# A two-layer attention, state-space and mixture kernel: the run-time loop over its batches written out

## The reference

```
x = x + attention(layernorm(x))      # A: linear attention, 16 heads of 8, a state that decays per token
x = x + mixture0(layernorm(x))       # B: top 2 of 8 experts, 352 hidden rows each, SiLU gated
x = x + state_space(layernorm(x))    # C: conv of width 3, selective scan with 16 states per feature, SiLU gate
x = x + mixture1(layernorm(x))       # D: top 2 of 8 experts, 128 hidden rows each, and 2 shared experts
```

## Time and profile before

| what | value |
|---|---|
| median of 3 runs | 2598.52 us (2598.12 to 2598.66) |
| span of the profiled execution, first to last instruction | 2595.4 us |
| PE busy | 2081.9 us, 80% |
| DVE busy | 1865.9 us, 72% |
| POOL busy | 1347.7 us, 52% |
| ACT busy | 1134.1 us, 44% |
| a turn of the loop, 922.34 to 1229.58 us | 307.24 us |

### The profile page before, as it was taken

The page is one execution under the profiler, slowest core; times in us unless marked ns, Lnnn a source line. Parts: engine busy times, 40 slices in busy tenths (PEclk is TensorE's granted clock), DMA queues, the critical chain, the costliest instruction groups (busy, mean ns, idle before and its releaser), DMA issues.

```text
span 2595.4 us, 26854 instructions
## 1 busy us (share of the span) xinstructions
PE 2081.9 (80%) x6944; PEld 866.6 (33%) x6944; DVE 1865.9 (72%) x3076; ACT 1134.1 (44%) x1491; POOL 1347.7 (52%) x848
## 2 busy tenths in 40 slices
PE   3589787789779987798877897878877998787468
PEld 1234332334323333233333343333332333332023
DVE  5655569775895859866697757967589676974972
ACT  1133374325644265243652347432663427535324
POOL 4346358453583537644485444745368353862343
PEclk8789899899898998899998999889988999988579
DMA  4000000000000000000000000000000000000000
GB/s 129 0 9 1 9 1 1 1 1 17 1 1 1 1 18 1 1 1 2 17 1 1 1 2 17 1 1 1 18 1 1 1 1 9 0 1 0 0 0 17
DMA packets 24911, 18.10 MB, mean 7 GB/s; under 512 B 2704, under 2 KB 23984, under 8 KB 24496
## 3 DMA queue, kind: packets, MB, share of 16 engines
q1 hardware_dynamic: 24752, 16.23, 2.0%
HBM read 12.04 MB, written 4.19 MB: 6 GB/s over the span
## 4 chain that ended last, share of the span: by engine, by line
PE 45%; issue 20%; DVE 17%; POOL 9%; ACT 7%; DVEq 1%; POOLq 0%; DMA 0%; ACTq 0%; SPq 0%
PE bank L920 10%; PE bank L780 7%; PE bank L782 7%; PE bank L781 6%; POOL mix_arena L746 4%; DVE arena L1303 4%; DVE arena L1314 3%; POOL arena L717 3%; PE bank L908 2%; PE bank L843 2%; DVE arena L1247 2%; PE bank L824 2%; DVE arena L1294 2%; POOL y L727 2%; PE bank L791 2%
## 5 line engine op out<-in xcount | busy, mean ns | idle before, releaser
L746 POOL TENSOR_TENSOR mix_arena<-mix_arena 128x512 f32<-128x512 f32 (+1 forms) x512 | 816.3, 1610 | 691.9 <-ACT mix_arena L1100 690.9
L1388 DVE SCALAR_TENSOR_TENSOR mix_arena<-bank,winv,mix_arena 128x512 f32<-128x512 f32 (+1 forms) x544 | 403.6, 744 | 436.0 <-PE bank L782 353.1
L1113 ACT ACTIVATE mix_arena<-bank,winv 128x512 f32<-128x512 f32 (+1 forms) x544 | 372.6, 687 | 575.3 <-PE bank L782 565.0
L920 PE MATMUL bank<-mix_arena,W_Bw 128*128 128x512 f32 (+1 forms) x768 | 432.9, 649 | 0.0
L727 POOL TENSOR_TENSOR y<-y,arena 128x1024 f32<-128x1024 f32 x120 | 284.1, 2367 | 199.2 <-DVE arena L1314 199.1
L1303 DVE TENSOR_TENSOR_SCAN arena<-arena 128x1024 f32<-128x1024 f32 x128 | 383.6, 2996 | 0.1
L780 PE MATMUL bank<-x_partsB,W_hi 128*128 128x512 f16 x712 | 298.7, 420 | 99.1 <-DVE mix_arena L1388 40.5
L876 PE MATMUL bank<-bc_parts,sel_bc 96*128 96x512 bf16 x512 | 198.4, 429 | 204.3 <-DVE arena L1314 162.4
L1100 ACT COPY mix_arena<-bank 128x512 f32<-128x512 f32 x256 | 149.6, 584 | 447.9 <-PE bank L908 447.7
L782 PE MATMUL bank<-x_partsB,W_lo 128*128 128x512 f16 x712 | 296.1, 416 | 0.0
L781 PE MATMUL bank<-x_partsB,W_hi 128*128 128x512 f16 x712 | 294.0, 413 | 0.0
(11 more groups left out here) (168 smaller groups left out, 2649.0 us busy)
## 6 DMA issues: line engine op xcount, KB each, us to landing
x<-in_x SPq DMA_DIRECT2D x8, 512.0 KB, 4.1
out<-x SPq DMA_DIRECT2D x8, 512.0 KB, 3.2
mix_arena<-in_W SPq DMA_DIRECT2D x2, 1408.0 KB, 8.4
W_Bw<-in_W SPq DMA_DIRECT2D x2, 512.0 KB, 14.2
mix_arena<-in_W SPq DMA_DIRECT2D x1, 640.0 KB, 11.3
x<-in_W SPq DMA_DIRECT2D x1, 640.0 KB, 12.4
W_Dw<-in_W SPq DMA_DIRECT2D x1, 640.0 KB, 4.9
x<-in_Wv SPq DMA_DIRECT2D x1, 512.0 KB, 4.4
```

The lines of the kernel that those rows point to most:

```text
L746: pool.tensor_tensor(slot, slot, g_ring[0:rows, q % RG, :], ALU.mult).then_inc(m_sg[s].sem, 1)
L920: last = pe.matmul(banks[4][:], W2[s][0:rows, i, :], h_ring[0:rows, k % RH, :], start=(i == 0), stop=(i == NT[s] - 1))
L1113: read(s, act.activation(s_ring[0:rows, k % RS[s], :], bank(s, f"a{k}", rows), ACT.Silu, scale=down[W1[s]][0:rows]))
L1388: read(s, dve.scalar_tensor_tensor(out=h_ring[0:rows, k % RH, :], in0=bank(s, f"b{k}", rows), scalar=down[W3[s]][0:rows], in1=s_ring[0:row ...
```

## The change

Both loops become Python loops, so that the body stands five times in each stream and every count is a constant:

```diff
-            with eng.Fori(1, B - 2) as i:
+            for i in range(1, B - 2):
                 ssm_beside(e, i, "B", i + 1, counts(A=i + 2, B=i + 1, C=i, D=i, PB=i + 2, PD=i), ("D", i),
                            ("D", i - 1), ("A", i + 2))
                 attention_beside(e, i + 2, "D", i, counts(A=i + 2, B=i + 2, C=i + 1, D=i, PB=i + 2, PD=i + 1),
...
             next_x(0)
             next_x(1)
-            with sp.Fori(0, B - 3) as b:
+            for b in range(0, B - 3):
                 store_x(b)
                 next_x(b + 2)
             for b in range(B - 3, B):
```

## The result

The kernel after takes 2571.71 us, median of four runs (2568.12 to 2572.78), against 2598.59 before (2598.12 to 2601.89): a ratio of 0.9893, 95% interval 0.9879 to 0.9907. The profiled execution (2568.12, span 2566.3) is the fastest of the four, 29.1 us off the profiled span of before.

What follows compares the result with a forecast made beforehand. No engine was full; PE and DVE waited for each other at every tile. Returns 10.3 plus registers 8.2, fetch and SP 0, gave 18.5 us off: 2598.5 - 18.5 = 2580.0 us, own range 2576 to 2583.5, with rivals 2575 to 2589.

Steps and rivals of the forecast that it cites:

- Part 1: Return to the loop's head, taken four times: 2.57 us each at the next mark, 10.3 us saved.
- J to N: From end of previous turn's gates (L1373) to the convolution's SiLU (L1042): 17.87 us with return, forecast 15.05 in turns 1 to 5.
- whole-turn figure: Turns 2 to 5 against turn 1, 307.18 against 303.98 us: 3.2 per return, upper bound 12.8.
- only the branch counts: Rival at the loop's head: a return costs only its branch, 0.3 us for four; 2590 us, chance 0.05.
- Part 2: Register instructions computing the waits' counts in the loop: 1.64 us a turn, 8.2 us over five.
- N to G: From the convolution's SiLU (L1042) to the product y times z (L1320): registers cost 0.90 us a turn.
- G to J: From the product y times z (L1320) to the gates' end (L1373): 139.69 to 139.20 us, 0.49 a turn.
- Part 3: Fetching the longer straight code instead of the loop: cost 0; a late fetch would cost 2.9 us.
- Part 4: SP's loop of one store and one load a turn: worth 0, upper bound under 0.2 us.
- Only the returns: Rival for the loop: register instructions are hidden, 10.3 to 12.8 us off, say 2587 us, chance 0.18.
- The clock: Something between, anywhere in the turns: a saving given back through a lower granted clock or different phase, chance 0.05.
- No DVE gap: Sign at the turns' borders: no DVE gap put down to issue at L1388, previously 2.92 us.

Runs made afterwards that it cites:

- m_pe: Kernel before with PE's stream written out, constants and no return; DVE, ACT and POOL keep loop and registers: 2597.87 us, ratio 0.9991.
- m_dve: Kernel before with DVE's stream written out, constants and no return; PE, ACT and POOL keep loop and registers: 2580.09 us, ratio 0.9926.
- e2_hint: Kernel before, loop and registers kept, with a hint to fetch the loop's head ahead: 2583.63 us, ratio 0.9938 to the kernel before.
- r_pe: Kernel after with counts computed in registers on PE alone, in once-run loops, no returns: 2586.43 us, ratio 0.9944 to the kernel before.
- e1_reg: Kernel after with counts computed in registers on all engines, each turn a once-run loop, no returns: 2585.84 us, ratio 0.995 to the kernel before.
- p10: Kernel after with DVE clearing 960 scratch columns at the end of turns 1 to 4: 2569.15 us, ratio 0.9878 to the kernel before.
- pb07: Kernel after with 0.75 us of DVE scratch clearing behind L1282 in turns 1 to 5: 2565.57 us, ratio 0.9877 to the kernel before.
- fill_b: Kernel before with 14 zero-weight products on PE where it idles for POOL in the attention scan: 2591.85 us, ratio 0.9972.
- r_ap: Kernel after with counts computed in registers on ACT and POOL alone, no returns: 2563.73 us, ratio 0.9885 to the kernel before.
- p28: Kernel after with DVE clearing 2700 scratch columns at the end of turns 1 to 4: 2607.77 us, ratio 1.0037 to the kernel before.

## Why the prediction was wrong

The direction, the order of the parts and the mechanism at the border were right; the size was not, and it fell outside the range.

**Part 1, returns.** The mechanism holds: fetch of the target, DVE's gap above PE's (m_pe has 17.7 to 18.0 us from J to N, m_dve 16.5 to 16.6), 2.57 us at mark N. J to N saved 11.2 us over the five turns where 10.3 + 1.25 were forecast. What was mis-sized is the step from a mark to a turn: the term 4 x 2.57 = 10.3 measured 13 to 16 by the ratios. The whole-turn figure, 3.2 and at most 12.8 in all, was there and I kept it as a bound; e2_hint's turn is 3.4 us shorter than that of before, and its time 16 us. The rival that only the branch counts, with 0.3 us for four returns, falls by the same 16 us.

**Part 2, registers.** Forecast 8.2, measured 12 to 15. The failed step is that turn 0 was the reference for code without registers. N to G was to fall by 0.90 and fell by 2.0 a turn, G to J by 0.49 and fell by 1.1. Turn 0 was one draw: W to S15 there took 111.4 us before and 113.9 after, A0 to A15 45.0 and 42.7, with instructions that are the same. A reference that itself moves by over 2 us in a stretch can't price 0.9. What stands without doubt is the 0.5 a turn in N to W and S15 to G for all engines together, 2.5 us; the rest appears in the two scans, where the clock's drops stand. Of these the attention scan is shown to follow the clock, 1.3 a turn; for the state-space scan, 1.5 a turn, that is not shown. The bounds were taken from DVE's ALU_OPs of two lines alone, 205 a turn; with ALU_OP and FUSED_REGOPS of all lines DVE has 364 a turn and PE 341. PE's registers, which I had listed and not priced, give some 13 alone (r_pe), and DVE's alone some 9: the two don't add.

**Part 3, fetch.** Right: DVE has no idle time above 0.5 us put down to issue in the kernel after, so nothing took the place of the returns. From 618 to 2151 us after, the instruction queues brought

```profile
q8 instruction: 36, 0.59, 0.2%
q14 instruction: 41, 0.34, 0.1%
```

which is 77 blocks where the earlier trace rows led to 80. **Part 4, SP:** not tried alone; m_pe, in which SP's loop is written out too, takes the time of before, so it is worth 5 us at most, PE's constants included.

**The rivals.** "Only the returns" (2587) is e1_reg's and e2_hint's time, but not this kernel's. The clock was given five chances in a hundred, and only as a way to lose a saving. The saving about doubled in the two scans: J to N and the stretches around the scans give 11.2 + 1.5 of the 26.5 in the turns, the scans 13.8, of which 6.4 are the attention's and so the clock's. Its range should have been taken on both sides, since the earlier trace rows already had turns with the same instructions 0.9 us apart. No step of the prediction foresaw that this would be a gain and not a loss.

**The marks.** No DVE gap: right. No ALU_OP at L88 and L74: right. J to N 15.05: 15.1. G to J 139.2: 138.4 in turn 2, 139.9 in turn 5. Turn 302.5 to 303.0: 300.3 to 303.0.

**Open.** Why the clock's drop at W comes earlier with PE's registers than without, from 0.2 us of delay; how much of W to S15 is the clock's; why the steady lengths are 300.4, 303.8, 307.2 and 310.7, and why other kernels (m_dve, p10, pb07) have none; and what W to S15 gave back in fill_b. A pad at W on PE would be the next look. No version is clearly faster than the kernel after: r_ap's and pb07's intervals overlap with its own.

## What to carry to other kernels

Price a loop's return at the next mark and at the whole turn, and take the second where PE's clock changes within a turn; here a prefetch hint (0.9938) gave back as much as code without returns (0.995). Never take one stretch elsewhere in the kernel as the reference for an edit of under 1%: look first at how far equal stretches lie apart, and put that into the range on both sides. Before a change of "issue" in the view of waits is called a cost, place the instruction against the last common mark.

## What the runs showed of the hardware

- A small edit can be worth several times its own time. 3.55 us of DVE work a turn made turns 3 to 5 of p28 about 10 us longer (310.3 to 310.8 against 300.4), 7.7 of them from J to N, where the granted clock stood at 0.54 for 7 us. 1.25 us a turn cost nothing (p10).
- Where turns repeated they were within 0.5 us of one another, at lengths 3.4 us apart: 300.3 to 300.5 (turns 2 to 4 of after), 303.7 to 304.2 (e2_hint, r_pe), 307.1 to 307.3 (turns 2 to 5 of before and m_pe), 310.3 to 310.8 (turns 3 to 5 of p28). Not every kernel settles: m_dve alternates between some 304.2 and 300.0.
- Between its first and last L1247 the attention took 42.7 us where the clock stayed up behind PE's idle time of 3.6 to 3.7 us (turn 0 of after), 43.5 where it was 0.75 over 6.8 us there (turn 2 of after), and 45.1 where it was 0.50 (turn 2 of before).
- A backward branch with a prefetch hint took PE 341 ns instead of 3687, and DVE's idle time behind its own was 0.70 us instead of 2.92.
